# A fused decoder on one core: two head groups per output strip, one PSUM bank per phase, the prelude inside the instruction plan, at most four batches under way

## The reference

```python
x = x + linear_attention(layernorm(x))           # phase 0: 16 heads, causal, elu(q)+1, elu(k)+1
x = x + attention(layernorm(x), ctx, key_mask)   # phase 1: 16 heads, 512 keys
x = x + top2_of_8_experts(layernorm(x))          # inside chain "to2"
x = x + attention(layernorm(x), window of 128)   # phase 2: 16 heads, 256 keys
x = x + differential_block(layernorm(x), ctx)    # phase 3: 8 heads, 512 keys, then norm, relu ffn, norm
x = x + ternary_linear(gelu(ternary_linear(layernorm(x), w_up)), w_down)   # chain "end"
# ternary weights: sign(w) * (|w| > 0.5 * mean(|w|))
# softmax(scores) @ v per head; outputs of all heads joined, then @ Wo + bias
```

## Time and profile before

| | |
|---|---|
| median of 3 runs | 1060.52 us (1055.59 to 1060.76) |
| the profiled execution | 1054.23 us, of which the span is 1052.5 us |
| PE busy | 848.7 us, 81% |
| DVE busy | 666.6 us, 63% |
| ACT busy | 488.6 us, 46% |
| POOL busy | 321.2 us, 31% |
| mean granted TensorE clock | 0.914 of full speed |

### The profile page before, as it was taken

One profiled execution on the slowest core, in us unless ns is written; L12 is line 12 of the kernel. 1 busy time (PEld: TensorE's weight loads), 2 busy tenths in 40 slices (PEclk: granted clock), 3 DMA queues, 4 the chain that ended last, 5 costly groups with the idle time before them and its releaser, 6 DMA issues.

```text
span 1052.5 us, 19620 instructions
## 1 busy us (share of the span) xinstructions
PE 848.7 (81%) x6455; PEld 475.7 (45%) x6522; DVE 666.6 (63%) x2234; ACT 488.6 (46%) x1017; POOL 321.2 (31%) x872
## 2 busy tenths in 40 slices
PE   0477786999999887989999877897999977866763
PEld 0344553443444543545555435674544444422452
DVE  6767556878777774777676757765678473533511
ACT  0432332655555553557666545365655625413331
POOL 6423333212132232224452224352421213320312
PEclk9788988999999998999999989799999998857875
DMA  6287876031230534345330447328140114233000
GB/s 193 60 157 158 179 175 132 20 54 30 42 69 5 107 92 84 71 81 106 52 83 26 66 89 155 54 95 127 34 71 4 48 21 84 74 64 63 2 6 5
DMA packets 124965, 79.85 MB, mean 76 GB/s; under 512 B 8312, under 2 KB 122176, under 8 KB 124736
## 3 DMA queue, kind: packets, MB, share of 16 engines
q1 hardware_dynamic: 124864, 78.59, 36.9%
HBM read 43.99 MB, written 32.90 MB: 73 GB/s over the span
## 4 chain that ended last, share of the span: by engine, by line
PE 45%; DVE 17%; DMA 13%; issue 7%; SPq 6%; POOL 6%; ACT 5%; DVEq 0%; another core or an unknown queue 0%; POOLq 0%; ACTq 0%
PE ob L1211 7%; PE mb L1153 6%; DMA cT<-ctxT_dram 5%; PE eb L1181 4%; PE side L1074 3%; PE eb L1182 3%; PE side L1082 3%; DMA bounce<-scratch 2%; DMA QW<-bounce 2%; PE side L1027 2%; DVE junk L1635 2%; PE side L1065 2%; PE side L1094 2%; DMA QP<-mrow 2%; DVE mx L1643 2%
## 5 line engine op out<-in xcount | busy, mean ns | idle before, releaser
L1365 ACT ACTIVATE probs<-eb 128x512 f32<-128x512 f32 (+1 forms) x512 | 274.8, 568 | 217.5 <-PE eb L1182 91.5
L1635 DVE CUSTOM_DVE_ANT_0 junk<-mb,maskq_add 128x512 bf16<-128x512 f32 x256 | 169.1, 688 | 49.0 <-PE mb L1153 37.4
L1211 PE MATMUL ob<-probs,V 128*32 128x256 f32 (+1 forms) x2048 | 133.3, 379 | 5.1 <-ACT probs L1365 2.2
L1643 DVE TENSOR_REDUCE mx<-mb 128x1 f32<-128x512 f32 x128 | 83.5, 685 | 56.1 <-PE mb L1153 53.7
L1181 PE MATMUL eb<-maskk_add,identb 128*128 128x512 bf16 x256 | 98.1, 383 | 9.7 <-issue 6.6
L964 POOL TENSOR_SCALAR nm<-mx 128x8 bf16<-128x8 f32 x80 | 20.1, 251 | 277.1 <-DVE mx L1635 117.9
L1153 PE MATMUL mb<-KS,QP 128*128 128x512 bf16 x227 | 81.3, 386 | 12.0 <-DVE mx L1635 6.9
L1182 PE MATMUL eb<-QP,KS 128*128 128x512 bf16 x231 | 88.3, 382 | 0.0
L1211 PEld LDWEIGHTS ob<-probs,V 128*32 128x32 f32 x2048 | 55.4, 111 | 65.6 <-issue 32.1
L874 POOL TENSOR_SCALAR rstd<-mv 128x2 f32<-128x2 f32 x64 | 16.5, 258 | 209.0 <-DVE mv L1431 207.8
L1374 ACT COPY OT<-ob 128x512 f32<-128x512 f32 x56 | 32.8, 585 | 73.4 <-PE ob L1205 44.0
(11 more groups left out here) (189 smaller groups left out, 1707.4 us busy)
## 6 DMA issues: line engine op xcount, KB each, us to landing
QP<-bounce SPq DMA_DIRECT2D x48, 256.0 KB, 5.5
KS<-bounce SPq DMA_DIRECT2D x32, 384.0 KB, 7.2
bounce<-scratch SPq DMA_DIRECT2D x48, 192.0 KB, 2.3
bounce<-scratch SPq DMA_DIRECT2D x64, 128.0 KB, 2.2
KS<-bounce SPq DMA_DIRECT2D x32, 192.0 KB, 6.0
bounce<-scratch SPq DMA_DIRECT2D x16, 384.0 KB, 2.6
cT<-ctxT_dram SPq DMA_DIRECT2D x16, 256.0 KB, 6.1
bounce<-scratch SPq DMA_DIRECT2D x16, 256.0 KB, 2.4
```

The costliest lines, as they stand in the source:

```text
L1211: ins = nc.tensor.matmul(bank[32 * j:32 * j + 32, S - n:S], v_of(core, kt, 4 * g + j), pr[:, (j % 2) * n:(j % 2 + 1) * n], start=(kt == 0) ...
L1365: nc.scalar.activation(probs[:, u % PROBS, 0:n], eb[:, u % 2, 0:n], ACT.Exp, scale=SCALE[core.p]).then_inc(probs_by[1], 1)
L1635: ins = V_.tensor_tensor_reduce(junk[:, e.n % 2, :], bank, maskq_add[:, t, :], 1.0, NEG_EXP, ALU.add, ALU.max, mx[slot][:, t, h:h + 1])
L1643: ins = V_.tensor_reduce(mx[slot][:, t, h:h + 1], bank, AX.X, ALU.max)
```

## The change

**Output strips.** In phases 0 to 2, V keeps heads 0 to 7 at columns 8 to 16 of a strip and heads 8 to 15 at columns 17 to 25. Groups g and g + 2 accumulate in the same strip and half bank, so that one bank holds a whole phase. The bank is kept once for each phase (32 copies to `OT` where there were 56), and "outputs" is four plain transposes of 128x128 in every phase. DVE reads the two column ranges with an instruction each.

**Prelude.** Its pieces are steps of the plan, with costs and needs, taken where an engine has nothing else. POOL signals after the identity and `own_max`, and makes the other constants later. ACT makes the two masks. The ternary weights are ten steps on POOL. SP issues its first loads in another order.

**Plan.** At most four batches are under way, `EARLY` is 12, PE's chain steps rank after turns but ahead of maxima, and the next core is chosen by batch minus phase.

```diff
-V_AT = (8, 8, 8, 0)
+V_AT = ((8, 17), (8, 17), (8, 17), (0,))
-EARLY, X_LANDS = 8, 9.0
+ACTIVE, EARLY = 4, 12
+X_LANDS, W_LANDS, ROWS_LAND = (3.6, 5.6, 6.2), 6.6, 11.0
+TERNARY = 10
+PRELUDE = {
+    "pool": [("values 0", 3.0, (), 0.0), ("forms", 2.6, (), 0.0), ("values 1", 3.0, (), 0.0), ("window", 2.4, (), 0.0), ("values 2", 3.0, (), 0.0)]
+            + [(f"ternary {i}", 1.3, ("alpha",), 0.0) for i in range(TERNARY)],
+    "act": [("masks", 2.4, (), 13.0), ("lambda", 0.3, (), ROWS_LAND), ("magnitudes", 1.4, (), 16.0)],
...
-    return [("pe", "outputs", (1.8, 1.8, 1.8, 1.0)[p], ()), ("pool", "biased", 0.75, ()),
+    return [("pe", "outputs", 0.65, ()), ("pool", "biased", 0.75, ()),
...
-RANK = {"turn": 1, "nm": 0, "row": 0, "max": 2, "exp": 3, "av": 4, "keep": 0.5}
+RANK = {"turn": -1, "nm": 0, "row": -1, "chain": 0, "keep": 0.5, "chain on TensorE": 1.5, "max": 2, "exp": 3, "av": 4}
...
-                found = [c for c in todo if c[2] <= t]
+                begun = len({r.b for r in runs}) - sum(r.name == "end" for r in runs)
+                found = [c for c in todo if c[2] <= t and (c[0] != "to0" or begun < ACTIVE)]
...
-                max_core = min(found, key=lambda c: (c.p, c.b))
+                max_core = min(found, key=lambda c: c.b - c.p)
...
-                exp_core = min(found, key=lambda c: (c.p > 0, max_cores.index(c) if c.p else c.b))
+                exp_core = min(found, key=lambda c: max_cores.index(c) if c.p else c.b)
...
-                chosen = ident[:].rearrange("p (h e) -> p h e", e=VW)[:, :, V_AT[p]:V_AT[p] + n]
                 for t in range(TQ):
-                    for g in range(GROUPS[p]):
-                        lo = (t * heads + 4 * g) * n
-                        ins = nc.tensor.matmul(bank[:, lo:lo + 4 * n].rearrange("p (h e) -> p h e", e=n), OT[o][:, g, t * P:(t + 1) * P], chosen,
-                                               start=True, stop=True)
+                    for half in range(2):
+                        ins = nc.tensor.transpose(bank[:, (2 * t + half) * P:(2 * t + half + 1) * P], OT[o][:, half, t * P:(t + 1) * P], ident[:])
...
-                pair = PAIRS_TO[core] - GROUPS[p] // 2 + g // 2
-                bank = ob[:, pair % OB, (g % 2) * S:(g % 2 + 1) * S]
+                turn_ = PHASES_TO[core] - 1
+                bank = ob[:, turn_ % OB, (g % 2) * S:(g % 2 + 1) * S]
+                first_, end = g == 0, g >= GROUPS[p] - 2
...
-                                               start=(kt == 0), stop=(kt == last), skip_group_check=True)
+                                               start=(first_ and kt == 0), stop=(end and kt == last), skip_group_check=True)
...
+                weight, over, under = w(("up", "down")[n]), tern[:, 0, :], tern[:, 1, :]
+                if step == 0:
+                    pool.wait_ge(alpha_ready, 1)
+                    link(G.tensor_scalar(over, weight, alpha[:, n:n + 1], None, ALU.is_gt))
+                elif step == 1:
+                    link(G.tensor_scalar(under, weight, -1.0, alpha[:, n:n + 1], ALU.mult, ALU.is_gt))
+                elif step == 2:
+                    link(G.tensor_tensor(over, over, under, ALU.subtract))
+                elif step == 3:
+                    link(G.tensor_tensor(over, over, weight, ALU.subtract))
+                else:
+                    ins = G.tensor_tensor(weight, weight, over, ALU.add)
...
+            def masks():
+                act.wait_ge(masks_in, 2 * 16)
+                nc.scalar.activation(maskq_add[:], maskq8, ACT.Copy, scale=NEG_MAX)
+                nc.scalar.activation(maskk_add[:], maskk8, ACT.Copy, scale=NEG_EXP).then_inc(masks_ready, 1)
...
-                    link(V_.reciprocal(r, o[:, :, hd]))
-                V_.tensor_tensor(An[l][:].rearrange("p t (h d) -> p (t h) d", d=hd), o[:, :, 0:hd],
-                                 r.unsqueeze(2).to_broadcast([P, m, hd]), ALU.mult).then_inc(an_ready[l], 1)
+                for j, at in enumerate(V_AT[p]):
+                    ins = V_.tensor_tensor(a[:, :, 8 * j:8 * j + 8, :], o[:, :, at:at + hd].rearrange("p (t h) d -> p t h d", t=TQ),
+                                           r[:, j, :].rearrange("p (t h) -> p t h", t=TQ).unsqueeze(3).to_broadcast([P, TQ, 8, hd]), ALU.mult)
```

333 lines of the change are left out of this document (186 added, 147 removed).

## The result

The changed kernel takes 984.51 us, median of 4 runs (980.8 to 989.74), against 1060.46 before: a ratio of 0.930, with an interval of 0.925 to 0.935. The forecast was 1009 with a range of 970 to 1048, so the sign and the range held and the forecast was 24.5 us too high. The profiled execution has a span of 979.7 us (1052.5 before) and a mean granted TensorE clock of 0.927 (0.914).

The account below looks back on a forecast made before the run. PE was taken as the bound from 172.4 to 345 us, idling mostly at both ends. 1054.2 - 17 (start) - 30 (outputs) + 4 (end) - 8 (middle) = 1003, scaled to a median of 1009 us; range 970 to 1048.

Parts of the forecast that it names:

- Start: From launch to the first exponential scores of phase 1: 52 us earlier less 35 of work put off, 17 us saved.
- Outputs: Four fp32 transposes per finish, paced by weight loads, save PE 35.6 us, 30 counted outside the start; bounds 17 to 36.
- whoever stands behind moves up: Reason for counting 30 us of outputs: PE's queue is in order and PE idles for other reasons than these products.
- My low bound by the chain: Outputs at the low end: if only what stands on the chain of waits counts, 17 us saved.
- End: After batch 7's phase 3 values: up to 6 us more PE work at a clock near 0.8, taken as +4 us.
- Middle: 870 to 949.5 us: phase 3 of batches 4 and 5 fills idle PE, 8 of 19.6 us back; other gaps unchanged.
- The sign that I named: In the new profile, an idle share of PE near 10% between 172 and 870 us.
- (b): Plan packs better everywhere: a third of PE's 93 idle us between 172.4 and 949.5 goes, 986 us; chance 0.15.
- (c): GpSimd and DVE exclude each other at the port, so ternary passes on POOL delay the start: 1021 us; chance 0.08.
- (d): Only what is on the chain counts and the start gives half: 22 us saved, 1038 us; chance 0.18.
- (e): Slower: PE waits for one chain where the first four batches give way to the last four, 1075 us; chance 0.12.
- (f): The change does what it says, but waits of the same size eat the gains: 1060 us; chance 0.05.

## Why the prediction was right, and where it wasn't

**Start: forecast 17, bounds 0 to 30.** PE's idle time in the first 200 us fell by 29.7, at the upper bound. The first half of the step held closely: first scores of phase 0 at 45.2 (forecast 45), the first stack at 37.15 (forecast 35), and the prelude alone was worth 17.5. The step that failed is the second half. I let the shorter transfers save 35 us and took 35 us off again for work that comes later. The first exponential scores of phase 1 came at 108.7, not 120, so 64 us earlier. With the rules of before, prelude and strips together, PE does 141.65 us of work in the first 200; with the new rules it is 156.65. The run with `ACTIVE` at 8 gives 17.9 us for the bound of four batches alone. I had counted it as a mere shift. In PE's work done at 200 us it is a gain.

**Outputs: forecast 30, bounds 17 to 36.** The count was right: 128 transposes in 20.5 us, where 384 and 64 products took 56, and four in 0.60 us. But my 0.56 us, four loads of 141 ns, is right by luck: the transposes follow each other after some 0.11 us, and the last one takes 0.27 us. The gain was 26 and 27 us in two settings. But the reason was wrong in part. PE's 27 us put back cost only 9 (0 to 18), so "whoever stands behind moves up" is true for about a third (at most two thirds), and ACT's copies, which I left at nothing, may be a few us. My low bound by the chain, 17, had the better view of PE's share. The full gain came close to the forecast of 30 by some luck, since something else seems to have been saved that I did not price.

**End: forecast +4.** PE's idle time for the last 47 us of work grew by 3.4. The chain at the end is the same chain.

**Middle: forecast 8, bounds 0 to 25.** The idle time fell by 5. The sign that I named, an idle share near 10% between 172 and 870, was missed: it is 12.9%. Here the mechanism was not seen at all. What the planner's rules change is the order, and with it also PE's busy time: I priced idle time alone, term by term, and took the busy time as a constant less the outputs. In the profiles, from the run with prelude and strips under the old rules (PE busy 832.6, idle 192.8) to the changed kernel (807.2, 172.5), 25.4 us of busy time go with the same products. At the lower level of the clock PE is busy for 139.4 and 94.0 us, which makes 22.7 of the 25.4. But these are the executions with the lowest and the highest clock of their fours. By the clocks of all of them the lower level held for 179 and 157 us on average, and an estimate from this gives the clock 11 us at most. Phase 0's scores beside maxima are a part of that and not the whole: in the late phases 0 PE is busy at the lower level for 16.3 us under the old rules and 6.7 in the changed kernel. Of the planner's 37 us, then, 15 are seen at the start and up to 11 in the clock, and the rest is not traced to a place.

Put as a sum, the runs say 17.5 (prelude), 26 (strips), and 37 (planner), with some 6 us counted twice. My sum had 12 for what the prelude brings to the start (17 less the outputs' 5), 35 for the strips, and 8 less 4 for the planner. The mis-sized term is the planner's: 4 forecast, 37 measured. That the time still fell into the range owes something to its width and to luck: 33 us too few for the planner and 5.5 for the prelude were partly made good by 9 too many for the strips and the 6 that are counted twice.

**The rivals.** (b), better packing, came nearest with 986, though not by its own mechanism: it took 31 us out of the idle time of the middle, and 5 went. (c), the port: pairs of DVE and POOL do slow each other down as before (below), but the ternary passes end at 53.1 and the keys' parts of `to1` of batch 0 begin at 54.57, after a wait for ACT, and the kernel with the passes on DVE was slower. Of the two pairs that the prediction showed for the rule, only the second is of its kind, two instructions that read SBUF; POOL's clear of V reads nothing. The rule of the Trainium skill that was cited for it ("SBUF — State Buffer", section "Who interferes with whom") did not turn the sign of this move. (d) falls with a gain of 75 us. (e), a gap where the first four batches give way to the last four, was not seen: PE waits at most 7.0 us in one piece between 60 and 950 us. A wait of 10.1 us stands in the run with `ACTIVE` at 8, near the end. (f) falls. But the run with the strips alone is the case that (f) and (e) describe: a saving turned into a loss by a fixed order that the saving itself had changed. I gave this 0.17 for the whole change, and for that part alone it happened.

## What to carry to other kernels

Where a planner writes the order, an edit of its costs is an edit of the order, and the order can be worth more than the edit: the same code took 1092 or 1036 us, by the order of phases. To price such a change, compare the orders of the large units (here the phases) first, look for stretches where all work at hand needs the same second engine (here phase 0's scores beside maxima, both for DVE; this accounts for a part of the loss in one run), and hold the order fixed when measuring a part. Busy time is not a constant: with the same instructions PE was busy 807 or 837 us in two profiled executions, by its clock. And a profile is one execution: compare the clocks of all of them before its busy time is put down to the edit.

## What was not expected of the hardware

In the first 20 us two of POOL's smallest instructions stretch beside DVE's clears. Timeline of the changed kernel, POOL, then DVE:

```profile
10.32 0.71 POOL L925 TENSOR_TENSOR rstd<-rstd,constant 128x2 f32<-128x2 f32 x1
11.12 0.24 POOL L937 TENSOR_SCALAR nshift<-mv 128x2 f32<-128x2 f32 x1
...
12.03 2.68 POOL L925 TENSOR_TENSOR rstd<-rstd,constant 128x2 f32<-128x2 f32 x1
14.79 3.71 POOL L937 TENSOR_SCALAR nshift<-mv 128x2 f32<-128x2 f32 x1
...
19.16 0.71 POOL L925 TENSOR_TENSOR rstd<-rstd,constant 128x2 f32<-128x2 f32 x1
19.96 0.24 POOL L937 TENSOR_SCALAR nshift<-mv 128x2 f32<-128x2 f32 x1
```

```profile
9.89 1.76 DVE L1466 MEMSET QP<- 128x2048 uint32 x1 [0.38 <-issue]
...
11.84 2.29 DVE L1463 CAST KS<-own_max 128x4096 bf16<-128x4096 f32 x1
14.51 1.76 DVE L1466 MEMSET QP<- 128x2048 uint32 x1 [0.37 <-issue]
16.19 2.23 DVE L1463 CAST KS<-own_max 128x4096 bf16<-128x4096 f32 x1
```

The same two instructions on two columns take 0.71 and 0.24 us where DVE does nothing (from 19.16 on), and also in the first pair, which lies within DVE's first clear of `QP` (9.89 to 11.65). In the second pair they take 2.68 and 3.71. The first of these began while DVE cleared `KS` (until 14.13) and ended at 14.71. The second ended at 18.50, just after DVE's last clear of `KS` (18.42). So the clear of `KS`, a cast, goes with both long times. The clear of `QP` doesn't by the first pair, yet the second long one began beside it, at 14.79, and didn't end before the cast that followed; why is open. DVE's first clear of `KS`, beside POOL's clear of V, took 3.85 us, and the later ones 2.29 and 2.23. A norm that needs POOL's root thus waited some 5 us for clears, in the very stretch where the start is decided. Moving the clears was not tried.
